# Graph layer with top-16 attention: who fetches one tile of source rows, and how a block's meta data is read

## What is computed

```python
    h = jnp.maximum(_layernorm(x, axis=-1), 0.0)
    Qv = h @ W_Q.T
    Ku = h @ W_K.T
    score = jnp.einsum('md,md->m', Qv[dst], Ku[src]) * (1.0 / np.sqrt(d))
    score = score * jnp.exp(-DECAY_LAMBDA * edge_dt)
    # per target node: keep the 16 edges of highest score, softmax over them (alpha)
    msgs = h[src_s] @ W_msg.T
    agg = jax.ops.segment_sum(alpha[:, None] * msgs, dst_s, num_segments=n)
    out = x + jax.nn.relu(h @ W_self.T + agg)
```

## Time and profile before

| | us |
|---|---|
| median of 3 runs (1989.3 to 1990.56) | 1989.38 |
| the profiled execution: its own time | 1988.18 |
| its span on the core | 1986.3 |
| busy: PE, DVE, ACT, POOL | 1400.6, 1485.4, 1073.6, 1473.9 |
| mean granted TensorE clock | 0.871 |

### The profile page before, as it was taken

How to read it: one execution, slowest core, us unless ns; L and a number is a source line. 1 busy time by engine, 2 the same in 40 slices (tenths; PEclk the granted TensorE clock), 3 DMA queues, 4 the chain that set the end, 5 groups by cost and what they waited for, 6 DMA issues and landing times. The chain is left out here.

```text
span 1986.3 us, 53501 instructions
## 1 busy us (share of the span) xinstructions
PE 1400.6 (71%) x15219; PEld 1282.7 (65%) x15220; DVE 1485.4 (75%) x5025; ACT 1073.6 (54%) x3376; POOL 1473.9 (74%) x1557
## 2 busy tenths in 40 slices
PE   1157889777777777677777777677777766777766
PEld 0057778767766667666666666676666666676665
DVE  7678999776877768677776777777776776777766
ACT  2767666545545455555545555455554545455553
POOL 7777777777777777777777777777777777777773
PEclk9968999887788888988888888978888889888988
DMA  8933333333333333333333333333333333333321
GB/s 232 288 105 93 118 103 119 104 89 103 91 101 97 95 103 90 103 90 102 96 95 104 89 103 92 100 103 88 103 90 102 92 99 103 88 104 93 96 74 32
DMA packets 125277, 207.20 MB, mean 104 GB/s; under 512 B 34569, under 2 KB 80821, under 8 KB 124767
## 3 DMA queue, kind: packets, MB, share of 16 engines
q0 software_dynamic: 49472, 101.49, 19.5%
q1 hardware_dynamic: 73278, 99.00, 15.4%
q10 hardware_dynamic: 2226, 3.25, 0.5%
HBM read 187.15 MB, written 17.25 MB: 103 GB/s over the span
## 5 line engine op out<-in xcount | busy, mean ns | idle before, releaser
L679 POOL DMA_INDIRECT X<-H_table,idx x653 | 619.2, 948 | 200.6 <-issue 195.4
L1206 ACT ACTIVATE X<-OT,w 128x125 f32<-128x125 bf16 x1792 | 530.0, 386 | 30.4 <-DVE w L1023 30.1
L1174 ACT ACTIVATE OT<-pT 128x512 bf16<-128x512 f32 (+1 forms) x500 | 275.2, 550 | 440.7 <-PE pT L1323 363.8
L679 POOL DMA_INDIRECT E<-H_table,idx x431 | 408.5, 948 | 132.2 <-issue 128.4
L679 POOL DMA_INDIRECT Z<-H_table,idx x398 | 377.7, 949 | 121.4 <-issue 118.7
L1323 PE MATMUL pT<-identb,O 125*128 125x128 bf16 x1800 | 213.1, 245 | 280.8 <-DVE X L944 231.2
L1323 PEld LDWEIGHTS pT<-identb,O 125*128 125x128 bf16 x1800 | 135.7, 109 | 333.1 <-issue 250.0
L1312 PE MATMUL pG<-G,O 125*128 125x128 bf16 x3600 | 318.9, 252 | 0.0
L1312 PEld LDWEIGHTS pG<-G,O 125*128 125x128 bf16 x3600 | 280.0, 116 | 0.1
L949 DVE TENSOR_REDUCE s<-X 128x8 f32<-128x1024 f32 x200 | 268.3, 1342 | 0.0
L1348 PE MATMUL pU<-X 128*128 128x125 f32 x1512 | 190.2, 281 | 1.5
(11 more groups left out here) (198 smaller groups left out, 2473.0 us busy)
## 6 DMA issues: line engine op xcount, KB each, us to landing
rawi<-D_table SPq DMA_DIRECT2D x50, 576.0 KB
ewt<-D_table SPq DMA_DIRECT2D x50, 576.0 KB
X<-H_table SPq DMA_DIRECT2D x792, 0.5 KB
X<-H_table,idx POOLq DMA_INDIRECT x653
E<-H_table SPq DMA_DIRECT2D x528, 0.5 KB
Z<-H_table SPq DMA_DIRECT2D x440, 0.5 KB
E<-H_table,idx POOLq DMA_INDIRECT x431
Z<-H_table,idx POOLq DMA_INDIRECT x398
```

The lines of the kernel that those rows point to most:

```text
L679: return eng.indirect_dma_start(out=Et[q][:, t * 128:(t + 1) * 128], out_offset=None, in_=x if b < RAW else H, in_offset=bass.IndirectOffs ...
L1174: AT.mark(eng.activation(OT[b % 3][:, q0[g]:q0[g] + GQ[g], :].rearrange("p t n -> p (t n)"), pT[:, 0:GQ[g] * 128], ACT.Copy), b, f"T{g}")
L1206: last = eng.activation(weighted(c)[:, t * 128:t * 128 + NB], OT[c % 3][:, t, 0:NB], ACT.Copy, scale=w[:, t:t + 1])
```

## The change

Four things change.

1. `EVERY` 4 to 3, `FROM` 20 to 18, `BYSP` 22 to 30, so `BYACT` 10 to 13, and `HEAD` 4 to 5. Owned are now 28 blocks: 18, 21, ... 99. Their rows are fetched over three passes, j = b - 4 to b - 2. SyncE takes 30 rows a pass, ScalarE 13, 13 and 12.
2. In SyncE's pass `own_numbers` stands behind `own_rows` instead of ahead of it, and takes the block's first edge from a register that `meta` has loaded.
3. `meta` loads the first edges of four blocks at once (`AT_ONCE`) and reads the three rows of META, which are now neighbours, with one transfer into 18 partitions of `MR`. TensorE turns the three parts with a transpose each.
4. The rows of META are numbered anew, in the set-up and in the rarely used path for heavy blocks too.

```diff
-    EVERY = 4
-    FROM = 20
-    BYSP = 22
+    AT_ONCE = 4
+    EVERY = 3
+    FROM = 18
+    BYSP = 30
     BYACT = -(-(128 - EVERY * BYSP) // EVERY)
-    HEAD = 4
+    HEAD = 5
...
-        MR = [sb(f"MR{q}", [128, 128]) for q in range(NM)]
+        MR = [sb(f"MR{q}", [T, 3 * 128]) for q in range(NM)]
...
                 PA.wait(eng, b - NM, "mT")
-                begins[b] = r = first_edge(mybir.EngineType.SP, b)
-                for k in (0, 2, 3):
-                    eng.dma_start(MR[q][32 * k:32 * k + T, :],
-                                  META[k, bass.ds(r, CAP)].rearrange("(t e) -> t e", e=128)).then_inc(s_mr[q], 16)
+                if b not in begins:
+                    n = min(AT_ONCE, B - b) if b >= LEAD + 2 else 1
+                    for k, r in enumerate(nc.values_load_multi_w_load_instructions(
+                            alrow[0:1, b:b + n], engines=[mybir.EngineType.SP], min_val=0, max_val=M,
+                            skip_runtime_bounds_check_because="a count of the M targets, rounded down")[1]):
+                        begins[b + k] = r
+                eng.dma_start(MR[q][:, :].rearrange("t (k e) -> t k e", k=3),
+                              META[0:3, bass.ds(begins[b], CAP)].rearrange("k (t e) -> t k e", e=128)).then_inc(s_mr[q], 16)
...
-                r = first_edge(mybir.EngineType.SP, b)
+                r = begins[b]
...
-                if owned(j + 2 + EVERY):
-                    own_numbers(j + 2 + EVERY)
                 b, k = share_of(j)
                 if b is not None:
                     own_rows(b, k)
+                if owned(j + 2 + EVERY):
+                    own_numbers(j + 2 + EVERY)
                 load_x(j)
...
-                PA.mark(eng.transpose(pA, MR[q][:, :], ident[:, :]), b, "mT")
+                for k, at in enumerate((0, 64, 96)):
+                    last = eng.transpose(pA[:, at:at + T], MR[q][:, k * 128:(k + 1) * 128], ident[0:T, 0:T])
+                PA.mark(last, b, "mT")
```

More of the change, by code:

```diff
@@ L378, in fetch @@
         def fetch(e, v):
-            for k in (0, 1, 3):
-                last = e.dma_start(FM[:, k:k + 1], META[k, bass.ds(v["e0"], 128)].rearrange("(p a) -> p a", a=1),
+            for k, row in ((0, 0), (1, 3), (3, 2)):
+                last = e.dma_start(FM[:, k:k + 1], META[row, bass.ds(v["e0"], 128)].rearrange("(p a) -> p a", a=1),
                                    allow_slow_non_contiguous=True).then_inc(s_fl, 16)
@@ L584, in _ @@
             for b in range(2):
-                eng.wait_ge(s_mr[b], 48)
+                eng.wait_ge(s_mr[b], 16)
             for c in range(1, NCH):
@@ L610, in _ @@
             for p, q in RUNS:
-                eng.dma_start(META[1, 0:M].rearrange("(p r) -> p r", r=RUN)[p:q, :], rawd[p:q, 1:]).then_inc(s_late, 16)
+                eng.dma_start(META[3, 0:M].rearrange("(p r) -> p r", r=RUN)[p:q, :], rawd[p:q, 1:]).then_inc(s_late, 16)
             for p, q in RUNS:
@@ L1099, in _ @@
             AS.wait(eng, "dec")
-            put(3, dec)
+            put(2, dec)
             VS.wait(eng, "pad")
@@ L1104, in _ @@
             VS.wait(eng, "slot")
-            put(2, stt[:, :])
+            put(1, stt[:, :])
             for p, q in RUNS:
@@ L1293, in prep_a @@
                 q = b % NM
-                eng.wait_ge(s_mr[q], 48 * (b // NM + 1))
+                eng.wait_ge(s_mr[q], 16 * (b // NM + 1))
                 VA.wait(eng, b - 1, "D01")
-                PA.mark(eng.transpose(pA, MR[q][:, :], ident[:, :]), b, "mT")
+                for k, at in enumerate((0, 64, 96)):
+                    last = eng.transpose(pA[:, at:at + T], MR[q][:, k * 128:(k + 1) * 128], ident[0:T, 0:T])
+                PA.mark(last, b, "mT")
             def turn(b):
```

## The result

The changed kernel takes 2011.67 us (median of 4, 2011.19 to 2014.07), the kernel before on the same chip 1989.7 us (median of 4). The ratio is **1.0114**, 95% interval 1.0101 to 1.0127: slower by 22 us where 5.6 us less were forecast, and outside the range of 1978 to 1996. The profiled execution took 2011.48 us, with a span of 2009.7 (1986.3 before).

What follows compares the result with a forecast made beforehand. GpSimd's gathers, 1.253 us each, were taken as the bound. The profiled 1988.2 - 10.0 (eight gathers) + 4.4 (GpSimd held at the start) = 1982.6, lying 1.2 under the median: 1983.8 us; range 1978 to 1996.

Steps and rivals of the forecast that it cites:

- Eight gathers, 10.0 us: On GpSimd: 28 owned blocks instead of 20 save 8 gathers of 1.253 us, 10.0 us, all on the path.
- SyncE's pass: On SyncE: passes of 16.9, 20.95 and 17.3 us, with limits 56.0 us for three, against GpSimd's 57.5.
- Register loads: On SyncE: loads of 30 numbers quick for k = 0 and 2 (2.3 us), slow for k = 1 (6.3 us).
- the 6.3 that the prediction calls the page's: Slow-loads rival: 30 numbers cost 6.3 us at each offset, SyncE 64.1 us for three passes, about 2155 us; chance 0.01.
- The turn of three passes: ScalarE's wait, k = 0 to fin, then SyncE's k = 1, k = 2 and limits: 56.2 us, below GpSimd's 57.5.
- the forecast wait for the new numbers: ScalarE starts the k = 0 pass no earlier than 5.3 us after SyncE's last row: landing about 2, load 3.3.
- The lag at pass 17: At the start of the owned blocks: the computation 13.7 us behind GpSimd at pass 17, 9.2 at pass 22.
- GpSimd held by U: Near blocks 22 to 24: GpSimd waits for ScalarE's U for 1.6, 1.5 and 1.3 us, 4.4 us in all.
- In the steady part this costs nothing: Requesting the next numbers behind SyncE's 30 rows keeps a turn at 56.2 us, below 57.5 by 1.3: no cost.
- the term of the meta transfer: In SyncE's pass: one meta transfer counted at 0.28 us, possibly 0.28 to 0.5, where three took 1.25.
- Set-up, "nothing": At the start: the first meta transfer lands at most 1 us earlier, for blocks gathered later; cost nothing.
- The slow rival: SyncE becomes the bound, 0.75 us more a pass, GpSimd held in 27 turns, some 30 us: 2009 us; chance 0.19.

Runs made afterwards that it cites:

- The version with both edits: Changed kernel with GpSimd's wait for its tile 1 landing moved from tile 5 to tile 8 and SyncE fetching 32 rows a pass: 1979.52 us, ratio 0.9943.
- the wait at tile 8: Changed kernel with only GpSimd's wait for its tile 1 landing moved from ahead of tile 5 to ahead of tile 8: 1990.89 us, ratio 1.0008.

## Why the prediction was wrong

**Eight gathers, 10.0 us: right.** 1536 against 1544 gathers, 1.25 us apart where nothing holds them. The version with both edits is 10.7 us faster than the kernel before, but that the two numbers are close is chance: there a quicker start (5.8 us) made up for holds and longer gathers.

**SyncE's pass: right.** The timeline of passes 15 and 16 (it answers to the earlier trace rows):

```profile
342.49 0.27 SPq L577 DMA_DIRECT2D xb<-in_x  x1
342.80 0.34 SPq L581 DMA_DIRECT2D out<-ob  x1
343.32 0.30 SPq L561 DMA_DIRECT2D MR<-META_table  x1
...
351.03 12.57 SPq L318 DMA_DIRECT2D X<-H_table  x30
363.65 0.27 SPq L577 DMA_DIRECT2D xb<-in_x  x1
...
369.64 12.21 SPq L318 DMA_DIRECT2D X<-H_table  x30
382.04 0.23 SPq L632 DMA_DIRECT2D own<-SRC_table  x1
382.32 0.27 SPq L577 DMA_DIRECT2D xb<-in_x  x1
```

One meta transfer 0.30 us (0.28 taken), 30 rows 12.57 and 12.21 (12.45), the pass of k = 1 21.16 (20.95), that of k = 2 with the load of four limits 18.67 (18.35; the limits took 1.4, not 1.05). Register loads were forecast at 2.3, 6.3 and 2.3 (they answer to the earlier trace rows):

```profile
L313 SPq TENSOR_LOAD <-own x84: 2224/2257/6304, 325.2 to 1937.0; - x84
```

The Trainium skill ("Runtime: NRT & Kernel Launch", Instruction fetch mechanics) has about 200 ns a register also in bulk: 6.304 / 30 = 0.21 us, the slow third of the loads, agrees with it; 2.257 / 30 = 0.075 us, the other two thirds, does not. (For 30 numbers the page's figure gives 6.0 us; the 6.3 that the prediction calls the page's comes from its own slow rows.) SyncE waited 40.1 us for fin, against 165.0 in the earlier trace rows.

**The turn of three passes: 1 us too short.** ScalarE at the start of passes 17 and 20 (it answers to the earlier trace rows):

```profile
386.64 0.28 ACT L1198 ACTIVATE Os<-pU 125x128 f32<-125x128 f32 x1 [6.92 <-issue]
386.82 0.27 ACT L1199 ACTIVATE Us<-pU 128x125 f32<-128x125 f32 x1
```

```profile
443.65 0.28 ACT L1198 ACTIVATE Os<-pU 125x128 f32<-125x128 f32 x1 [6.93 <-issue]
443.82 0.27 ACT L1199 ACTIVATE Us<-pU 128x125 f32<-128x125 f32 x1
```

Both passes begin with the forecast wait for the new numbers (ScalarE goes on 4.8 us behind SyncE's last row; 5.3 were taken), and 57.0 us lie between them, where 56.2 were summed and GpSimd needs 57.5. The lag at pass 17 is 387.1 - 377.7 = 9.4 us, not 13.7: SyncE began at 342.5, not 345. At pass 23 it is 7.7. A smaller lag that is worked off more slowly gave the same price: GpSimd held by U for 0.4, 1.0 and 2.5 us at blocks 23 to 25 and 0.6 at block 37, **4.5 us where 4.4 were forecast**. That agreement is of the sum, not of its terms. The longest of these waits:

```profile
522.07 0.94 POOL L684 DMA_INDIRECT X<-H_table,idx  x1 [2.81 <-ACT Us L1199]
```

**The step that failed: "In the steady part this costs nothing".** I asked of SyncE's later pass only whether U would be late for GpSimd, the wait that `in_step` makes. I had not put down another wait of GpSimd, `s_g` ahead of tile 5, since the kernel before never showed it. Its margin there can be read from the trace: tile 1 landed after 2.6 us in the median and 4.4 at most (blocks 20 to 97), where 4.2 are free. And I had taken SyncE's free time as slack with no content, when it also fixes *where the 576 KB go*. With it used up, the spread slid from 3 us ahead of tile 1 to 1.35 (median).

The other half is in the term of the meta transfer. I priced it by its issue alone (0.28 us) and the rest as "nothing". What stands behind it in SyncE's queue lands later, `hb` by 1.8 us, and the spread takes 5.0 us instead of 3.8.

Tile 1 now landed after 3.8 us in the median and 6.2 at most, and 24.3 us, more than twice the gain, were lost in waits of up to 2 us that bear the name "issue". The term missing in the sum is 23.7 us; with it the forecast would have been 2007.5.

**Set-up, "nothing": wrong by 2.8 us.** GpSimd's first gather of block 5 comes at 120.69 instead of 117.86. GpSimd's idle time at tile 5 of blocks 1 to 4 is 6.3 us before and 9.2 now. With the wait at tile 8 it is gone there, block 5 begins at 112.3, and 5.7 us come back as waits in blocks 6 to 8.

**The slow rival** (2009 us, chance 0.19) named the right time for the wrong reason. It wanted 0.5 us more in each pass of SyncE and GpSimd held by U turn after turn; SyncE's terms were as summed, and U holds GpSimd only in blocks 23 to 25 and 37. Luck, then, so far as it was right. What it had right is that SyncE's margin was thin.

**How far the cause is shown.** That the time is lost in the wait at tile 5 is shown by taking it away: ratio 1.0114 to 1.0008, and by the 0.78 us from landing to tile 5 in each late pass. That tile 1 lands late beside the spread is read from the traces of all six kernels (the table above): of the idle time at tile 5, 23.4 of 24.0 us in the changed kernel and 31.4 of 34.0 us with the spread behind the rows (blocks 20 to 97) stand in passes with the spread between 2 us ahead of tile 1 and 1 us behind. The Trainium skill ("DMA: Bandwidth & Descriptors", Queues, rings and completion order) says that each engine takes turns between its queues packet by packet; a gather that starts together with a large transfer on the same 16 engines would then end late, which fits.

How the 24 us divide between the spread's new place and its longer run behind the new meta transfer is open: no run changed the spread's size, and none had the old meta transfer with 30 rows where the kernel before takes 1989 us. It isn't the meta transfer alone: with the spread behind the rows there are 3 passes with the meta transfer less than 2 us ahead of tile 1 and the spread 4 to 6 us ahead, and tile 1 landed there after 2.6 to 2.8 us. Open too is why with 32 rows tile 1 takes 3.4 us also where the spread stands 4 to 6 us ahead, and with it the 10.2 us that this kernel still loses at tile 5.

## What to carry to other kernels

Before you spend an engine's slack, list what it issues and which landings those transfers run beside; slack is also the thing that keeps a large transfer out of the way of a small one that somebody waits for. For the engine that bounds the kernel write down every wait in its program with its margin, the silent ones too, and move each to the last place where it is still early enough for its readers: three tiles later took 21 us off here. A transfer that is given another shape has a second price beside that of its issue: look at when the transfers behind it in the same queue land. Where a helper's cost depends on a start position (register loads here), choose the split so that all positions are good ones.

## What the hardware showed that was not expected

- A register load of 32 numbers takes 2.05 us and one of 30 takes 2.25 or 6.30, by where it starts: at 0, 128 and 256 bytes, and at 0 and 240, it is quick, at 120 (and 88 and 264 before) slow. All quick starts are multiples of 16 bytes, and no slow one is.
- A gather of 128 rows of 512 bytes lands 2.5 us after its start (median) when 576 KB were issued 4 to 6 us ahead of it, and after 5.3 us, 6.2 at most (block 74), when they were issued within 1 us of it.
- One transfer of 54 rows of 512 bytes for three of 18 issues in 0.30 us instead of 1.25, but a transfer of 125 rows right behind it lands 4.4 us after its issue instead of 2.6, and the 576 KB behind that take 5.0 us instead of 3.8.
- Some 37 us hung on the place of one transfer in SyncE's queue (2049.3 against 2011.7), partly because a small request behind it landed late.
- The same program takes 1.68 times as long in some of the runs, with the same time for a gather; SyncE's instructions, register instructions too, are there 0.70 us apart in stretches of some 18 us.
